# One block for all turns: barriers and semaphore clears between batches replaced by waits on running counts

## The reference, cut to what matters

```
xn  = layernorm(x)
q, k, v = xn@Wq, xn@Wk, xn@Wv          # 16 heads of 16, 8 key/value heads
mask = causal & (within 128 tokens | key is a landmark)
       # landmark: among the top 33% of a score of the token's norm and its
       # likeness to the batch's mean, spread to two neighbours on each side
s   = softmax(q k^T / 4 + mask) v @ Wo
h   = gelu(xn @ sign(w1)^T + b1)        # sign() with a dead zone, 1024 wide
g   = silu(h @ sign(w2)^T + b2)
out = x + s * g
```

## Time and profile before

| | us |
|---|---|
| median of 3 runs | 663.1 (663.02 to 665.38) |
| the profiled execution's own time | 661.63 |
| its span in the profile | 660.0 |
| PE busy | 567.8 (86%) |
| ACT busy | 446.9 (68%) |
| DVE busy | 408.2 (62%) |
| POOL busy | 265.0 (40%) |

### The profile page before, as it was taken

How to read it: one execution, slowest core, us unless ns; L and a number is a source line. 1 busy time by engine, 2 the same in 40 slices (tenths; PEclk the granted TensorE clock), 3 DMA queues, 4 the chain that set the end, 5 groups by cost and what they waited for, 6 DMA issues and landing times. The chain is left out here.

```text
span 660.0 us, 10907 instructions
## 1 busy us (share of the span) xinstructions
PE 567.8 (86%) x3729; PEld 293.0 (44%) x3729; DVE 408.2 (62%) x915; ACT 446.9 (68%) x576; POOL 265.0 (40%) x306
## 2 busy tenths in 40 slices
PE   0669499999999889999899699999898799899983
PEld 0657145343435455443444355444444465224522
DVE  5889577877476477968485377968485544511122
ACT  4335777876787547876777567876777667798660
POOL 3424633334426333343435253343426353254441
PEclk9969799999999789999999799999999899799997
DMA  8002442121322343011232243011231243011001
GB/s 247 0 1 70 125 116 72 32 62 25 99 60 60 107 104 94 28 57 33 75 83 54 72 143 97 27 52 39 60 94 53 57 145 93 24 59 43 23 15 37
DMA packets 50675, 45.18 MB, mean 68 GB/s; under 512 B 9036, under 2 KB 44988, under 8 KB 50620
## 3 DMA queue, kind: packets, MB, share of 16 engines
q1 hardware_dynamic: 49468, 43.61, 23.8%
q10 hardware_dynamic: 1152, 0.85, 0.5%
HBM read 11.41 MB, written 4.19 MB: 24 GB/s over the span
## 5 line engine op out<-in xcount | busy, mean ns | idle before, releaser
L1617 ACT ACTIVATE f_probs<-sc_ps,shift 128x1024 f32<-128x1024 f32 (+3 forms) x384 | 332.7, 900 | 108.4 <-PE sc_ps L1515 102.3
L1515 PE MATMUL sc_ps<-f_q_stack,f_k_stack 104*128 104x512 bf16 (+3 forms) x768 | 196.0, 346 | 31.5 <-ACT f_probs L1617 16.0
L1532 PE MATMUL att_ps<-f_probs,f_v_sb 128*32 128x512 f32 (+3 forms) x1536 | 167.8, 511 | 6.2 <-POOL f_probs L1681 6.2
L1674 POOL TENSOR_SCALAR_AFFINE_SELECT f_probs<-f_probs 128x512 f32<-128x512 f32 x128 | 94.8, 741 | 134.7 <-ACT f_probs L1617 134.4
L1515 PEld LDWEIGHTS sc_ps<-f_q_stack,f_k_stack 104*128 104x128 bf16 x768 | 48.5, 99 | 196.2 <-ACT f_probs L1617 119.5
L1681 POOL TENSOR_TENSOR f_probs<-f_probs,f_near 128x512 f32<-128x512 f32 x64 | 77.8, 1215 | 133.9 <-ACT f_probs L1617 133.9
L1452 PE MATMUL aux_ps<-w2T,f_h_hi 128*128 128x256 f32 x256 | 71.9, 314 | 0.0
L1661 POOL TENSOR_TENSOR f_h_lo<-f_hid,f_h_hi 128x512 fp32r<-128x512 f32 x36 | 47.1, 1317 | 43.9 <-DVE f_h_hi L1739 43.9
L1452 PE MATMUL aux_ps<-w2T,f_h_lo 128*128 128x256 f32 x256 | 62.8, 278 | 0.0
L1532 PEld LDWEIGHTS att_ps<-f_probs,f_v_sb 128*32 128x32 f32 x1536 | 31.1, 109 | 69.2 <-issue 44.8
L1729 DVE TENSOR_TENSOR f_probs<-f_probs,f_near 128x512 f32<-128x512 f32 x48 | 36.7, 764 | 31.4 <-ACT f_probs L1617 30.4
(11 more groups left out here) (204 smaller groups left out, 729.7 us busy)
## 6 DMA issues: line engine op xcount, KB each, us to landing
f_q_stack<-f_q_parts SPq DMA_DIRECT2D x192, 64.0 KB
f_k_stack<-f_k_parts SPq DMA_DIRECT2D x96, 64.0 KB, 2.2
xn<-in_L_attn_hidden_states SPq DMA_DIRECT2D x4, 1024.0 KB, 6.7
f_attT<-f_att_raw SPq DMA_DIRECT2D x126, 32.0 KB
f_rden_bc<-f_den SPq DMA_DIRECT2D x60, 64.0 KB
s_w_nat<-in_L_ffn_w SPq DMA_DIRECT2D x2, 1024.0 KB, 9.4
f_x_res<-in_L_attn_hidden_states SPq DMA_DIRECT2D x4, 512.0 KB, 4.9
out_y<-f_x_res SPq DMA_DIRECT2D x4, 512.0 KB, 3.2
```

The lines of the kernel that those rows point to most:

```text
L1515: last = pe.matmul(sc_ps[:, 2 * u + hh, lo:CH], k_stack[0:KROWS + T, h // REP, kb * P:(kb + 1) * P], q_stack[0:KROWS + T, SLOT[n], 2 * u + ...
L1532: last = pe.matmul(att_ps[32 * q:32 * q + 32, n % 2, lo:CH], v_sb[:, kb, j * VW:j * VW + 32], probs[:, i % NPROB, q, lo:CH], start=(kb == ...
L1617: act.activation(probs[:, i % NPROB, us, lo:CH], sc_ps[:, us, lo:CH], ACT.Exp, bias=shift[:, 0:1], scale=HD ** -0.5).then_inc(exp_done, 1)
L1674: pool.affine_select(out=block_probs, in_=block_probs, compare_op=ALU.is_ge, fill=0.0, base=0, pattern=[[0, NQ], [1, P]], channel_multipli ...
```

## The change

There is one block for all five turns. `turn` no longer opens a block: it returns five functions, one for each engine, and each engine calls those of all turns one after the other. The loop over batches 1 and 2 is written out. Each wait gets the count that its semaphore had reached when the turn began (`into`), from a table of gains by kind of turn. Where a turn's start relied on the barrier, a wait on data is added: PE waits for `kstack_in`, `q_in`, the last exponentials, free banks, `hid_split` and `hid_split_pool`; SP for `xT_done`, `dots_done`, `hid_split`; DVE for `att_in`; ACT for `pv_done`, `gate_done`. SP's waits at a preparing turn's end go, and so do the four clears between turns with both their barriers.

```diff
+ gains = ((kstack_in, 208, 400, 400), (q_in0, 112, 336, 336), ...
+ def turn(b, main, prep, prev, x_next, reached):
+     def into(sem, n):
+         return reached[sem.num] + n
...
-                    with nc.Block(no_gpsimd_drain=True) as block:
-                        @block.sync
-                        def _(sp):
+                    def sp_turn(sp):
...
                             spread_rden(0)
+                            sp.wait_ge(hid_split, into(hid_split, 0))
+                            sp.wait_ge(hid_split_pool, into(hid_split_pool, 0))
                             sp.dma_start(x_prev[:, :, :], xp[:, TC:T, :]).then_inc(xprev_in, 16)
+                        sp.wait_ge(xT_done, into(xT_done, 0))
+                        if prev:
+                            sp.wait_ge(dots_done, into(dots_done, 0))
                         if prep:
                             sp.dma_start(xn[:, :, :], x_next.rearrange(...)).then_inc(x_in, 16)
...
-                                sp.wait_ge(hid_split_pool, FT)
-                                for slot in range(3):
-                                    sp.wait_ge(q_in[slot], 16 * (NPART + 1) * (...))
-                                sp.wait_ge(kstack_in, 16 * (NPART * (GROUPS if main else 2) + 1))
...
-                                    if t >= TC:
-                                        pe.wait_ge(hid_split, FT // 2)
-                                        pe.wait_ge(hid_split_pool, FT // 2)
+                                if t >= TC or prev:
+                                    pe.wait_ge(hid_split, into(hid_split, FT // 2 if t >= TC else 0))
+                                pe.wait_ge(hid_split_pool, into(hid_split_pool, FT // 2 if t >= TC else 0))
...
+                            if i == 0 and u == 0:
+                                pe.wait_ge(kstack_in, into(kstack_in, 0))
...
-                                if i >= 1:
-                                    pe.wait_ge(exp_done, 2 * (i - 1) + u + 1)
+                            if i >= 1 or prev:
+                                pe.wait_ge(exp_done, into(exp_done, 2 * (i - 1) + u + 1))
...
-                    clear_semaphores()
-                turn(None, False, True, False, None)
-                turn(0, True, True, False, x[1])
-                with nc.Fori(1, B - 1) as b:
-                    turn(b, True, True, True, x[b + 1])
-                turn(B - 1, True, False, True, None)
+                reached = {sem.num: 0 for sem in sems}
+                for kind, args in [...]:
+                    parts.append(turn(*args, dict(reached)))
+                    for sem, *gain in gains:
+                        reached[sem.num] += gain[kind]
+                with nc.Block(no_gpsimd_drain=True) as block:
+                    @block.tensor
+                    def _(pe):
+                        for _, pe_turn, *_ in parts:
+                            pe_turn(pe)
...
+                clear_semaphores()
```

More of the change, by code:

```diff
@@ L1621, in _ @@
                                 for j in jobs_at(i - 0.5, i):
                                     job(*j)
-                                if main and i in TANH_AT:
-                                    half_tanhs(TANH_AT.index(i))
-                                if main:
-                                    exps(i)
+                                if i < NSTEP:
+                                    scores(i, 0)
+                                if i >= BEHIND:
+                                    values(i - BEHIND)
@@ L1627, in _ @@
+                                if i < NSTEP:
+                                    scores(i, 1)
                                 for j in jobs_at(i, i + 0.5):
                                     job(*j)
-                            if main:
-                                tail = jobs_at(NSTEP - 0.5, 999)
-                                first = [j for j in tail if j[1] == "ffn_up"]
-                                for j in first:
-                                    job(*j)
-                                if prep:
-                                    act.activation(bound[:, 0:1], shift[:, :], ACT.Exp)
-                                for j in tail[len(first):]:
-                                    job(*j)
-                                if not prep:
-                                    act.wait_ge(att_out, NG)
-                                    for q in range(2, NQ):
-                                        row = ((H - NQ) % HT + q) * HD
-                                        act.dma_start(attT[row:row + HD, QT - 1, :], att_raw[32 * q:32 * q + HD, :]).then_inc(att_in, 16)
-                            else:
-                                act.activation(bound[:, 0:1], shift[:, :], ACT.Exp)
@@ new lines, in turn @@
+                    return sp_turn, pe_turn, act_turn, pool_turn, dve_turn
+                reached = {sem.num: 0 for sem in sems}
+                parts = []
+                for kind, args in [(0, (None, False, True, False, None)), (1, (0, True, True, False, x[1]))] + \
+                                  [(2, (b, True, True, True, x[b + 1])) for b in range(1, B - 1)] + [(2, (B - 1, True, False, True, None))]:
+                    parts.append(turn(*args, dict(reached)))
+                    for sem, *gain in gains:
+                        reached[sem.num] += gain[kind]
@@ new lines, in fast_path, with _ @@
+                with nc.Block(no_gpsimd_drain=True) as block:
+                    @block.sync
+                    def _(sp):
+                        for sp_turn, *_ in parts:
+                            sp_turn(sp)
+                    @block.tensor
+                    def _(pe):
+                        for _, pe_turn, *_ in parts:
+                            pe_turn(pe)
+                    @block.scalar
+                    def _(act):
+                        for _, _, act_turn, *_ in parts:
+                            act_turn(act)
+                    @block.gpsimd
+                    def _(pool):
+                        for *_, pool_turn, _ in parts:
+                            pool_turn(pool)
+                    @block.vector
+                    def _(dve):
+                        for *_, dve_turn in parts:
+                            dve_turn(dve)
```

1158 lines of the change are left out of this document (590 added, 568 removed).

## The result

| | before | after |
|---|---|---|
| median of 18 runs each | 664.33 us (661.97 to 666.54, and one of 1328.18) | 656.25 us (653.13 to 662.70) |
| ratio | | 0.9898, 95% interval 0.9877 to 0.9918 |
| profiled execution: time, span, granted clock | 661.63, 660.0, 0.952 | 657.62, 652.9, 0.961 |

The kernel is 1.0% faster by the ratio, and 8.1 us (1.2%) by the two medians; 656.5 was forecast. One run of the kernel before took twice as long as the others; without it the median is 664.25. Of the changed kernel's runs 13 took 653.1 to 657.6 us and five 660.5 to 662.7. No trace of one of the five was kept, so what they lose stays open.

A forecast was written before the change was run, and what follows sets the result against it. PE was 86% busy, but no engine runs through: PE and ACT hand heads back and forth. Seams -9.8, batch 1 -1.25, batch 2 +3.5, waits +1.0 sum to -6.6 us, median 656.5; range 651.5 to 660.5.

The forecast's parts named there:

- Seams: The four places between turns where barriers and clears stood: idle time there goes, 9.8 us gained in sum.
- The first seam: Preparation to batch 0: PE's scores wait only for the landmarks' rows and start at about 74.8, 1.2 us gained.
- a start later than 75: Sign of being wrong: batch 0 starting later than 75 us in the profile.
- the cover is thinner: Rival, chance 0.17: xn delays the landmarks' rows at batch 0, or all 70 waits are exposed; about -3.5 us, 659.6.
- What is late next: The load of xn in batches 1 and 2: batch 1 improves by 1.25 us, batch 2 loses 3.5.
- about 147.5 in both: Sign: batches 1 and 2 each last about 147.5 us from first exponentials to last value copy.
- the clock stays up: Rival, chance 0.22: PE keeps its high clock at the stalled matmuls, both stalls 1.5 us smaller; -9.6, 653.5.
- the term of 1.0: Some 70 extra waits on PE cost 1.0 us, between none and 3.5.
- the profiled execution took 661.63 with a span of 660.0; so span 653.4 and time 655.0: Summing step: -6.6 us on the profiled execution; the runs' median, 1.5 above it, then gives 656.5.
- No stall comes back: Rival, chance 0.03: xn arrives early enough in batches 1 and 2; -13.4 us, 649.7.
- the gaps are replaced by waits: Rival, chance 0.10: the seams show the new waits at the old times; within 0.5%, 659.8 to 666.4.
- PE's instruction supply: Rival, chance 0.06: PE meets 3.4 us gaps in the written-out straight code; three beyond the one removed make it 666.7, slower.

The follow-up runs named there:

- barrier_after_preparation: The changed kernel with one barrier put back behind the preparation, batches 0 to 3 staying in one block: 655.22 us, ratio 0.9864 to the kernel before.
- waits_four_times: The changed kernel with PE's waits for hid_split and hid_split_pool before each half of a down projection issued four times: 658.70 us, ratio 0.9926 to the kernel before.
- empty_block_first: The changed kernel with an empty block, so one more barrier, ahead of the block that holds everything: 655.36 us, ratio 0.9858 to the kernel before.
- barrier_0_to_1: The changed kernel with one barrier put back between batches 0 and 1: 657.44 us, ratio 0.9903 to the kernel before.

## Why the prediction was right

**Seams: right.** Batches 0 to 1, 1 to 2 and 2 to 3: 1.5, 5.4 and 1.7 were forecast; ACT's gaps of 1.56, 5.44 and 1.72 became -0.15 each, 1.7, 5.6 and 1.9 gained. The first seam gave the 1.2 too, measured from the issue of the landmarks' rows: 7.04 us to the exponentials before, 5.88 after. In absolute time PE started at 75.96, though, and I had named a start later than 75 as a sign of being wrong. The rows landed 4.9 us behind their issue (4.7 forecast), with `xn` right behind them, so the full sharing of bandwidth didn't come, and "the cover is thinner" falls with it. The rest is that they were issued 1.0 later. Most of that, 0.88, was there at the end of `set_up`, in code that the change doesn't touch; DVE's first row behind its barrier, before and after:

```profile
32.96 0.09 DVE L1898 MEMSET f_count<- 128x32 f32 x1 [1.33 <-PEq L181]
```

```profile
33.84 0.09 DVE L1916 MEMSET f_count<- 128x32 f32 x1 [2.33 <-PEq L181]
```

Over all profiles this row starts between 32.83 and 34.29, and the kernel before alone spans most of that (32.96 and 34.29). So the later start isn't the change's doing, and "later than 75" was a poor sign of being wrong.

**What is late next: right in size, by two errors that cancel.** Batch 2 lost the 3.5 us forecast (144.1 to 147.6 from first exponentials to last copy), batch 1 gained 1.8 (1.25 forecast); "about 147.5 in both" came out as 146.8 and 147.6. The mechanism is shown by three kernels: written out, the loop gives batch 2 the stall; `xn` ahead of the spreading takes it from both. But `xn` landed later than I had it: DVE's statistics 12.49 and 13.32 us behind the first exponentials instead of 12.15, a wait of 4.8 to 4.9 instead of at most 4.5. In batch 2 the issue came 0.8 later than in batch 1. And the 1.5 us of low clock, which I had taken in each, wasn't there: that was the mechanism of the rival "the clock stays up". It isn't a fixed property of the change, though. Four more kernels have the changed kernel's seam ahead of batch 2 and its place of `xn`. In the profiles of three (`barrier_after_preparation`, `waits_four_times`, `empty_block_first`) batch 2 and its seam took 148.4 to 148.7 us instead of 147.4, with the low clock; in that of `barrier_0_to_1` 146.95, without it. So that the changed kernel's one profile has the high clock twice is luck in part. PE's eight matmuls behind the wait in batch 2, in `empty_block_first`, and in `barrier_0_to_1`:

```profile
381.13 2.90 PE L1470 MATMUL aux_ps<-wo_sb,f_attT 128*128 128x256 f32 x8 [1.93 <-DVEq L1779]
```

```profile
384.32 1.99 PE L1470 MATMUL aux_ps<-wo_sb,f_attT 128*128 128x256 f32 x8 [1.48 <-DVEq L1779]
```

Over all profiles these matmuls took 1.99 us in the six rows where PE had stood for 0.97 to 1.85 us before them, and 2.90 to 3.78 us in the ten where it had stood for 1.93 to 4.48. The changed kernel's 1.75 in batch 2 is near the upper end of the six, so a load that lands some tenths later would, by these rows, likely cost it another microsecond. What else decides the clock here wasn't tried.

**Batch 0: missed.** It took 1.6 us more from first exponentials to last copy (143.2 against 141.6), where only extra waits were reckoned. Aligning DVE's copies of the sums, of which each batch has eight, puts 0.8 before the first copy, where PE's values ran 1.51 us instead of 0.85 in the low clock, and 0.7 at 149 to 151 us, where ACT waits for the `q_stack` fills: SP needed 5.71 us instead of 5.17 for eight DMA issues ahead of them. Batches 1 and 2 don't have it, which speaks against the waits. Most of the 1.6 differs from execution to execution: in the nine other profiles with the changed kernel's waits batch 0 took 141.6 to 143.1 us, in the other three of kernels with the waits of before 141.7 to 142.7. `waits_four_times`, with the most waits, has 142.1, with 5.18 us for the eight issues and 1.06 for the values. Batch 3's gain of 1.04, which the prediction had at nothing, isn't explained either: over all profiles the stretch from its first exponentials to the end took 138 to 140.

**Waits: the term of 1.0 stands, weakly.** See above. In the profile no stretch of the middles of batches 1 and 2 got longer: within each, from DVE's second copy of the sums on, all later ones keep their distance from before to within 0.4 us.

**The step that failed: "the profiled execution took 661.63 with a span of 660.0; so span 653.4 and time 655.0".** It adds 1.63 us outside the span, unchanged. It became 4.72 in the profiled execution and 4.4 in the median. And the profiled span of before was 1.6 to 2.3 below the median span of its runs (661.6 to 662.3 by round). By medians the change took 9.9 to 10.6 us off the span, where 6.6 were forecast, and put 2.4 to 2.7 back outside it. The gain in time was 8.1 us; 656.5 came out because the median of before, 663.1 in three runs, was 664.33 in 18. So the total was right by luck: these errors cancel, as well as the two in the stall. A reader should take the seams and the stall from the prediction, and not the precision of its total.

**Rivals.** "No stall comes back", "the gaps are replaced by waits": no row for either. "PE's instruction supply": no gap inside the written-out code. Its sort of stop exists elsewhere, at the end: the branch over the fallback, when fast path and span end. Its rows in the changed kernel, and PE's in the kernel before (durations minimum, median, maximum):

```profile
L2020 DVEq COMPARE_BRANCH  x2: 56/56/57, 33.7 to 649.0; - x2
L2020 PEldq COMPARE_BRANCH  x2: 90/1978/3867, 33.7 to 649.0; - x2
```

```profile
L1972 PEldq COMPARE_BRANCH  x2: 90/1924/3757, 32.8 to 656.3; - x2
```

PE stands in it for 3.87 us while the others take some 0.05. The kernel before has it too (3.76), so it is no cost of the change. The Trainium skill (Runtime: NRT & Kernel Launch, "Instruction fetch mechanics") says that a taken branch to code that isn't at hand makes the engine fetch it first. The trace agrees in kind; that the fetch is what takes the 3.87 us no run here shows.

## What to carry to other kernels

Before taking out a barrier or a branch, look at what arrives behind it: here removing the loop's branch alone gave back all of the seam's 3.8 us, and a little more, as a wait for a load whose place in the queue hadn't changed, and moving that load ahead of eight small DMAs was worth 4.6 us in the kernel without barriers but 2.6 in the one with them. A barrier's price is not only its own gap (1.2 us here), since it also sets where the following loads and PE's clock stand. Compare medians of times and of spans apart, and take more than one profile before a term of 1 us is believed.

## What the runs showed that I had not expected

- The time outside the span isn't a constant: 1.65 to 2.0 us in the medians of nine kernels (single executions 1.5 to 2.4), 3.2 to 4.8 (2.8 to 5.3) in the four whose turns stand in one block with no barrier ahead of it.
- `xn`, 1 MB, issued at the same place of batch 2, landed after 6.5 to 7.9 us in six kernels and after 9.0 and 9.6 in the two that have a barrier there and no loop. In batch 1 of these two it took 7.3 and 7.0, so a barrier alone doesn't do it. The cause is open.
- PE's compare-and-branch at the end took 3.3 to 4.2 us in all profiles, before and after, about as long as at the loop's end before (3.36), against about 0.05 on the other engines.
